# VectorE's own ordering in the edge stage: pipe drains in the place of semaphores that VectorE raises and waits for itself

## The reference

```python
# graph layer
h = layernorm(x)
neigh = segment_sum(h[src], dst, num_segments=12500)   # 200,000 edges
h = (1 + eps) * h + neigh
h = relu(h @ W1 + b1) @ W2 + b2                        # 256 -> 512 -> 256
x = x + batchnorm(h) * gamma + beta
# expert layer: top-1 of 8 experts, capacity 1.25
t = layernorm(x)
probs = softmax(t @ gate_w + gate_b); idx = argmax(probs)
x = x + prob * expert_ffn[idx](t)                      # 256 -> 1024 -> 256
```

## Time and profile before

| what | value |
|---|---|
| median of three runs | 3169.5 us |
| lowest and highest run | 3138.97 and 3172.03 us |
| span of the profiled execution | 3175.1 us |
| DVE busy | 1442.5 us (45%) |
| POOL busy | 1710.4 us (54%) |
| PE busy | 1826.2 us (58%) |
| first and last gather issue (line 791) | 118.0 and 2285.7 us |

### The profile page before, as it was taken

How to read it: one execution, slowest core, us unless ns; L and a number is a source line. 1 busy time by engine, 2 the same in 40 slices (tenths; PEclk the granted TensorE clock), 3 DMA queues, 4 the chain that set the end, 5 groups by cost and what they waited for, 6 DMA issues and landing times. The chain is left out here.

```text
span 3175.1 us, 32785 instructions
## 1 busy us (share of the span) xinstructions
PE 1826.2 (58%) x9046; PEld 1097.7 (35%) x9047; DVE 1442.5 (45%) x4225; ACT 694.9 (22%) x1116; POOL 1710.4 (54%) x1690
## 2 busy tenths in 40 slices
PE   0154444455545455655554455564568768989995
PEld 0022212222222222322222222232357645566664
DVE  8765511543225422531252112122336557786885
ACT  6600000000010001000100001110046554636642
POOL 0366664655645565555644444445315556767874
PEclk9976667676767677777877777777776688999997
DMA  7533354324633354234423332212246432222220
GB/s 244 188 104 106 116 184 138 106 88 132 197 101 91 115 182 148 87 121 144 152 65 121 120 111 65 67 54 79 54 145 216 131 93 75 71 84 73 79 83 18
DMA packets 201521, 361.08 MB, mean 114 GB/s; under 512 B 62117, under 2 KB 125947, under 8 KB 201334
## 3 DMA queue, kind: packets, MB, share of 16 engines
q0 software_dynamic: 69152, 185.00, 19.3%
q1 hardware_dynamic: 130038, 172.60, 16.8%
q10 hardware_dynamic: 2144, 1.05, 0.1%
HBM read 291.08 MB, written 71.92 MB: 114 GB/s over the span
## 5 line engine op out<-in xcount | busy, mean ns | idle before, releaser
L791 POOL DMA_INDIRECT halves<-table,halves x1240 | 1187.7, 958 | 1011.5 <-issue 367.1
L879 PE MATMUL e_sums<-halves 128*128 128x256 f16 x1920 | 334.7, 346 | 392.8 <-issue 244.1
L1062 DVE SCALAR_TENSOR_TENSOR nodes<-e_sums,above,nodes 128x256 f32 (+1 forms) x161 | 77.3, 480 | 967.0 <-remote 437.4
L879 PEld LDWEIGHTS e_sums<-halves 128*128 128x128 f16 x1920 | 229.6, 122 | 508.3 <-issue 425.7
L936 PE MATMUL e_up<-e_hT,W1s 128*128 128x512 f32 (+1 forms) x400 | 229.8, 734 | 234.9 <-ACT e_hT L985 140.2
L985 ACT ACTIVATE e_hT<-e_up 128x1024 f32<-128x1024 f32 (+1 forms) x25 | 25.2, 1007 | 1524.0 <-remote 1185.3
L1720 POOL TENSOR_TENSOR x_midl<-x_midf,x_midh 128x512 f16<-128x512 f32 x200 | 298.7, 1517 | 104.9 <-ACT x_midh L1854 99.4
L917 PE MATMUL e_tally<-w1f,counts 128*128 128x512 f16 x490 | 165.5, 480 | 281.6 <-DMA w1f<-table 204.9
L1126 DVE TENSOR_TENSOR counts<-counts,e_tally 128x490 f32 x220 | 159.8, 726 | 267.8 <-PE e_tally L907 147.9
L1810 PE MATMUL x_down<-halves,x_midh 128*128 128x256 f16 x1472 | 249.4, 277 | 16.6 <-DVE x_yb L1947 15.0
L1786 PE MATMUL x_up<-x_xTh,halves 128*128 128x512 f16 (+1 forms) x800 | 233.6, 371 | 3.1 <-ACT x_midh L1854 3.1
(11 more groups left out here) (208 smaller groups left out, 2752.4 us busy)
## 6 DMA issues: line engine op xcount, KB each, us to landing
w1f<-table SPq DMA_DIRECT2D x120, 512.0 KB
halves<-table,halves POOLq DMA_INDIRECT x1240
slot_rows<-halves SPq DMA_DIRECT2D x64, 268.0 KB
x_row<-slot_rows SPq DMA_DIRECT2D x32, 536.0 KB, 7.4
table<-halves SPq DMA_DIRECT2D x25, 512.0 KB, 2.9
counts<-in_x SPq DMA_DIRECT2D x24, 512.0 KB, 4.5
r_xin<-in_x SPq DMA_DIRECT2D x24, 512.0 KB
out<-r_row SPq DMA_DIRECT2D x24, 512.0 KB
```

The lines of the kernel that those rows point to most:

```text
L791: pool.indirect_dma_start(got[:, r, t, :], None, table.rearrange("p h d -> (p h) d"), bass.IndirectOffsetOnAxis(ap=idx[:, r, t:t + 1], axi ...
L879: ins = nc.tensor.matmul(sums[:, place, 0:D], hot[:, place, t, :], got[:, r, t, half * D:(half + 1) * D], start=(t == 0 and half == 0), st ...
```

## The change

In `stage_edges` VectorE's stream now has `dve.drain()` (the instruction DRAIN, which holds the sequencer until the engine's pipe is empty) where it waited for its own semaphores. The semaphores `s_rel`, `s_count` and `s_spread` are gone; `s_add` stays for PE. The drains stand in front of the comparisons (160), of the additions of sums (161), of the counts (220), of the folds (5), of each half of a spread (10) and of the copies of quads (25), 581 in all. In the loop and in the last addition, the drain stands in front of the wait for `s_sum`, in `gathered_once` behind it. No other engine's stream is changed, and no data instruction of DVE is added, removed or moved.

```diff
@@ gathered_once
                     nc.vector.tensor_scalar(rel[:, place, :], plan.cold[:, number * GT:(number + 1) * GT],
-                                            plan.least[:, at(number)], None, ALU.subtract).then_inc(s_rel, 1)
+                                            plan.least[:, at(number)], None, ALU.subtract)
                     word = dve.value_load(plan.words[0:1, at(number)], min_val=0, max_val=1 << 21)
                     shift = dve.snap(dve.snap(word // P) % P)
-                    dve.wait_ge(s_rel, number + 1)
+                    dve.drain()
                     for t in range(GT):
                         ins = nc.vector.tensor_scalar(hot[:, place, t, :], plan.ring[:, ring_at(shift)],
                                                       rel[:, place, t:t + 1], None, ALU.is_equal)
                     ins.then_inc(s_hot, 1)
                     dve.wait_ge(s_sum, number + 1)
-                    dve.wait_ge(s_add, number + 1)
+                    dve.drain()
                     add_window(1 - place, at(max(number - 1, 0))).then_inc(s_add, 1)
@@ gathered (the loop over windows)
-                                                ALU.subtract, ALU.subtract).then_inc(s_rel, 1)
-                        dve.wait_ge(s_rel, turn)
+                                                ALU.subtract, ALU.subtract)
+                        dve.drain()
...
                         ins.then_inc(s_hot, 1)
+                        dve.drain()
                         dve.wait_ge(s_sum, turn)
-                        dve.wait_ge(s_add, turn)
@@ count
                     dve.wait_ge(s_tile, OR + last_tile + 1)
-                    if group > 0:
-                        dve.wait_ge(s_count, group)
                     place = counts[:, :, bass.ds(column, TW)]
+                    dve.drain()
                     nc.vector.tensor_tensor(place, place, tally[:, group % BANKS, 0:KEY].rearrange("p (k d) -> p k d", d=TW),
-                                            ALU.add).then_inc(s_count, 1)
@@ fold
-                    dve.wait_ge(s_count, GROUP_OF[FIRST[u + 1] - 1] + 1)
+                    dve.drain()
@@ spread
-                    dve.wait_ge(s_add, turns)
                     for half in range(2):
+                        dve.drain()
                         for b, mask in ((0, plan.upper), (1, plan.lower)):
...
-                            then(ins)
```

More of the change, by code:

```diff
@@ L689, in stage_edges @@
         s_got = [sem(f"e_got{r}") for r in range(RG)]
-        s_hot, s_rel, s_sum, s_add, s_flush = sem("e_hot_s"), sem("e_rel_s"), sem("e_sum"), sem("e_add"), sem("e_flush")
+        s_hot, s_sum, s_add, s_flush = sem("e_hot_s"), sem("e_sum"), sem("e_add"), sem("e_flush")
         s_hrow, s_turn, s_hT, s_up, s_mid, s_down, s_h2 = (
@@ L693, in stage_edges @@
             sem("e_h2"))
-        s_tall, s_tile, s_count, s_fold, s_blank = (
-            sem("e_tall_s"), sem("e_tile"), sem("e_count"), sem("e_fold"), sem("e_blank"))
+        s_tall, s_tile, s_fold, s_blank = sem("e_tall_s"), sem("e_tile"), sem("e_fold"), sem("e_blank")
         s_part, s_used = [sem(f"e_part{h}") for h in range(2)], sem("e_used")
-        s_spread, s_cleared = sem("e_spread"), sem("e_cleared")
+        s_cleared = sem("e_cleared")
         s_pin, s_pgot, s_phot, s_psum, s_padd, s_pfree, s_prel = (
@@ L1055, in _ @@
                 last_group = counter(dve, "last_group", SINGLE - 1)
-                flushed = [0]
                 def add_window(place, group):
@@ L1104, in gathered @@
                         dve.reg_add(turn, turn, 1)
[L1106 to L1109, removed]
                 def one_hots(t):
@@ L1122, in count @@
                     dve.wait_ge(s_tile, OR + last_tile + 1)
-                    if group > 0:
-                        dve.wait_ge(s_count, group)
                     place = counts[:, :, bass.ds(column, TW)]
+                    dve.drain()
                     nc.vector.tensor_tensor(place, place, tally[:, group % BANKS, 0:KEY].rearrange("p (k d) -> p k d", d=TW),
-                                            ALU.add).then_inc(s_count, 1)
+                                            ALU.add)
                 def counted(t):
@@ L1142, in fold, with spread @@
                         count(group)
-                    dve.wait_ge(s_count, GROUP_OF[FIRST[u + 1] - 1] + 1)
+                    dve.drain()
                     wide = counts[:, :, 0:CW - P]
                     nc.vector.tensor_tensor(wide, wide, counts[:, :, P:CW], ALU.add).then_inc(s_fold, 1)
-                def spread(u, turns):
+                def spread(u):
                     first = dve.snap(dve.value_load(plan.unit[0:1, u:u + 1], min_val=0, max_val=N) // P)
                     dve.wait_ge(s_used, (u + 1) * (MIX * RG * PIECES + 1) + 2)
-                    dve.wait_ge(s_add, turns)
                     for half in range(2):
+                        dve.drain()
                         for b, mask in ((0, plan.upper), (1, plan.lower)):
                             row = blocks_of[:, block_no(dve.snap(first + b)), :].rearrange("p a d -> p (a d)")
-                            ins = nc.vector.scalar_tensor_tensor(
+                            nc.vector.scalar_tensor_tensor(
                                 out=row, in0=tally[:, BANKS - 1, half * D:(half + 1) * D], scalar=mask[:, u:u + 1], in1=row,
                                 op0=ALU.mult, op1=ALU.add)
-                            then(ins)
                 def measure(q, width=QN):
@@ L1163, in measure, with quad @@
                         nc.vector.bn_stats(stats[:, c, q * 6:q * 6 + 6], nodes[:, q, c * QN:c * QN + width])
-                def quad(q, turns):
+                def quad(q):
                     k = ORDER.index(q)
@@ L1183, in _ @@
                         if n in SPREAD and r == 0:
-                            spread(SPREAD[n], n * RG + 2 if n * RG < SINGLE else turn)
+                            spread(SPREAD[n])
                         for q in quads_at(n, r):
-                            quad(q, n * RG + r + 2 if n * RG < SINGLE else turn)
+                            quad(q)
+                dve.drain()
                 dve.wait_ge(s_sum, turn)
-                dve.wait_ge(s_add, turn)
-                then(add_window(dve.snap(dve.snap(dve.snap(turn) + 1) % 2), group_no(dve.snap(last_group))))
-                quad(NQ - 1, turn)
+                add_window(dve.snap(dve.snap(dve.snap(turn) + 1) % 2), group_no(dve.snap(last_group)))
+                quad(NQ - 1)
                 measure(NQ - 1, N - (NQ - 1) * QN)
```

## The result

In 20 runs of each kernel the kernel after took 3169.76 us in the median (3153.53 to 3200.75), the kernel before 3155.99 us (3122.79 to 3172.94). The ratio is 1.0069, with an interval of 1.0047 to 1.0091: slower by 14 us between the medians, 22 us by the ratio (15 to 29), and within one per cent. Executions over 1.5% above the fastest of their kernel, such as two of e6's twelve, count in the medians and not in the ratios. The two profiled executions show the opposite, 3159.9 us after and 3175.1 before. Single executions of one kernel lie up to 50 us apart, so two spans say nothing of a difference of this size.

A forecast was written before the change was run, and what follows sets the result against it. POOL's gathers, 1560 of 2168 us, were taken to set the stage's pace, DVE not. Costs of 4 + 5 + 1 = 10 us, less 2 to 3 for `rel` and spreads, gave 8 us on 3169.5: 3177 us, range 3145 to 3202.

The forecast's parts named there:

- What a drain does to DVE: DVE in the edge stage: drains add about 105 us of its time, between 25 and 150, not kernel time.
- (a): Behind a quad: comparisons and one to three counts come later, 0.3 us at each of 14 quads, 4 us.
- (b): In front of a quad: it starts up to 1.5 us later, 0.8 in the mean, 11 us; half counted, 5 us.
- Step (c): Last stage: DVE waits for PE there, so drains are covered; 1 us, 22 us at most without cover.
- Comparisons, quads, folds, spreads: DVE's time: comparisons 6 us, quads 5, folds and last addition under 2, spreads at most a microsecond in favour.
- Rival A: Among single-tile counts DVE becomes the bound and drains count 1:1: 3225 us, half of it 3197; chance 0.20.
- Rival B: Fewer semaphore increments shorten the "remote" pauses by a third, 36 us: 3134 us; chance 0.12.
- Rival C: All quads start into a pause, nothing reaches the path: 3165 to 3173 us; with forecast and D, chance 0.68.
- Rival D: A drain passes in 24 ns without holding the sequencer; time as before within 5 us; with forecast and C, 0.68.
- The sign to look for: POOL's waits for PE's sums (192.7 us): up by under 15 us confirms the sum, by 40 or more Rival A.

The follow-up runs named there:

- e6: Copy of the kernel after, timed beside the kernel before on the slower chip (the second comparison): 3163.7 us, ratio 1.0029 (0.999 to 1.0067).
- e4: Kernel before, no drains; counts also wait by semaphore for the one-hot row, additions for the comparisons directly in front: 2576.49 us, 1.0041 against before.
- e9: Kernel after plus two unused `bn_stats` in front of each of the 50 counts of the first 21 groups: 2582.69 us, 1.0083 against the kernel before.
- e3: Kernel after with counts and additions put back to their own semaphores, the other drains left: 2562.08 us, 0.9998 against the kernel before.
- e8: Kernel after plus one unused `bn_stats` in front of each of 157 counts away from quads, slower chip: 3190.51 us, 1.0166 against the kernel before.
- e10: Kernel after plus one unused `bn_stats` in front of each of 107 single-tile counts not near a quad: 2608.2 us, 1.018 against the kernel before.
- e1: Kernel before with drains instead of `s_count` in front of the 220 counts only: 2569.24 us, 1.0021 against the kernel before.
- e2: Kernel before with drains instead of `s_add` in front of the 161 additions of sums only: 2567.73 us, 1.0016 against the kernel before.
- e11: Kernel after plus two unused `bn_stats` in front of each of the 63 counts near quads: 2613.0 us, 1.0191 against the kernel before.
- e12: Kernel after plus two unused `bn_stats` between comparisons and addition in 95 windows without counts: 2584.86 us, 1.0083 against the kernel before.
- e5: Copy of the kernel before, unchanged, run once for a trace on the slower chip: 3127.93 us.

## Why the prediction was right, and where it was not

**The forecast.** Slower within one per cent was what came. The 8 us are met by the second comparison, 9 us (-3 to 21), and by the sum of parts on the faster chips, 9 us; in the first comparison it was 14 to 22 us, and its interval of 15 to 29 leaves 8 out. That 3177 us stands so near 3169.76 is luck in part: it starts from a median of three runs that lies 13.5 us above that of all twenty.

**What a drain does to DVE.** Each size was read off the rows of before, and held. Median gaps where DVE waited for no other engine, before and then with drain:

| place | before, us | with drain, us | difference | predicted |
|---|---|---|---|---|
| one-hot row to count | -0.08 | +0.18 | 0.26 | 0.25 |
| comparisons to addition | -0.08 | +0.21 | 0.29 | 0.25 |
| `bn_stats` to a quad's copy | -0.08 | +0.08 | 0.16 | 0.2 |
| `rel` to comparisons | 0.26 | 0.28 | 0.02 | 0.04 |

About half of the additions wait for PE's sum anyway. So 220 x 0.26 + 161 x 0.29 + 25 x 0.16 + 160 x 0.02 = 111 us at the most, against the 105 us of the prediction. DVE's busy time was said to stay nearly as before; it rose by 28 us, since instructions that no longer overlap are counted in full. That was left out.

The Trainium skill, page "VectorE: DVE Perf Modes", section "The DRAIN you can't avoid", says that a semaphore behind each instruction costs nothing extra, as the pipe is emptied between instructions anyway; it adds that an instruction that isn't held starts earlier. The runs agree with the addition and disagree with the rest: counts began 0.08 us before the end of the row in front, and e4, where a semaphore makes them wait for it, costs 1.0041 (1.0022 to 1.0061).

**What of it lies on the path.** Here the prediction's steps (a) and (b) failed in their reason, and that their sum of 9 us is near is luck. They price every quad alike, by the few drains just behind it (0.3 us) and just in front of it (up to 1.5 us, 0.8 in the mean, half of it swallowed). In the traces eleven of the fourteen quads cost nothing and those of groups 65, 108 and 114 cost 12 us together (e9 against e3). The step should have been: every count and addition between two quads lowers the rate at which lateness is made up, from 3.2 us in a group to 1.9 (10.1 less 6.9, and less 8.2, by the prediction's own numbers), and the quad that comes before it is made up hands on the rest, 8.2 us for the quad of group 65 (21.8 against 13.6). The place was right, then, and the amount came from the whole stretch in front of it. That larger doses cost as much far from the quads (e8, e10) is the other case, in which DVE is the bound.

**Step (c)**, 1 us for the last stage, was too small. From the first gather of group 120 to that of the last group it is 351.1 us in e3 and 351.0 in e1, which have no drains in front of additions, and 353.5 to 357.8 in e2, e9, e10 and e11, which have: 2 to 7 us, of the 22 that the drains could be at most there. e12, with its doses in the loop, takes 359.0.

**Comparisons, quads, folds, spreads**, at nothing to a few microseconds: right within 4 us; e3 is at 0.9998 (0.9981 to 1.0014).

**Rival A** had the mechanism: DVE among the single-tile counts, 8.2 us for a group in place of 6.9. Both numbers are in the traces (7.9 to 8.3 in e1, 6.7 to 7.3 in e3; in the kernel after 8.07 us, from 1014.75 to 1022.82, and 8.2 to 8.7 in e9's groups without doses). It also named what decides, the slack of the slot. But it priced the drains at 1:1 in the time from there on, and at 8.2 us against 10.0 the slack is built up again; the runs show most of a dose in the time only where a group reaches POOL's pace. e10 comes nearest to that price: 10.7 us for a group, and 0.6 of the dose in the time. At 8.2 us the share is 0.1.

**Rival B**, shorter pauses: "remote" 108.1 us before and 110.4 after, 105.7 and 101.8 in e5 and e6. Not seen. **Rival C**, no cost at all: excluded by the first comparison and by e1 and e2, though not by e6 alone. **Rival D**, a drain that doesn't hold: refuted by every gap.

**The sign to look for** was weak. POOL's waits for sums up by under 15 us would confirm, the prediction said. They went from 362.6 to 360.3 us in traces whose spans differ by 15 us the wrong way. The sign held, and says nothing; on a faster chip it would have been worth more, as the table shows.

No experiment pointed to a version that beats the kernel before. The best, e3, is no different from it.

## What to carry to other kernels

An ordering on the engine's own results is cheap as long as it names a result several instructions back, and dear when it waits for the one directly in front: 0.26 to 0.32 us each here, by a drain or by a semaphore alike. What that costs the kernel depends on how fast the engine makes up for a stall: compare its time for one unit of work in an unbroken run (7.9 to 8.7 us here) with the pace of the engine that sets the stage (10.0 us), and see whether the next stall comes before the last is made up. Well below that pace a tenth of the time was paid here, above it half or more.

## What the runs showed of the hardware that was not expected

Two chips gave 2564 us for the kernel before and a third gave 3150 us. The gathers in e3 (a faster chip; its time is that of the kernel before) and then in e5 (the slower chip), with what POOL waited for in front of them:

```profile
L791 POOL DMA_INDIRECT halves<-table,halves x1240: 942/949/1350, 118.0 to 1701.7; - x178
...
  issue: 363.8, 1188
  DMA halves<-rows_of: 36.0, 8
  PE e_sums L879: 14.7, 36
```

```profile
L791 POOL DMA_INDIRECT halves<-table,halves x1240: 940/946/1492, 116.5 to 2242.6; - x178
...
  issue: 363.0, 1157
  PE e_sums L879: 181.7, 19
  PEq L901: 177.6, 16
  remote: 134.6, 38
```

A gather takes the same time on both, and the pace between two is the same (363.8 and 363.0 us of issue). The waits differ: for sums 25.4 us (14.7, and 10.7 of PE's sequencer) and 359.3, "remote" none and 134.6, for the index loads 36.0 and 113.4. Together that is 546 us, the whole of the 542 us by which the gathers take longer. Neither the kernel nor the change makes this. The granted clock was 0.840 and 0.781 of full speed; PE's matmuls of line 936 took 604 and 729 ns and had 28.3 and 201.9 us of idle in front of them, so that a quad is longer there. What the "remote" pauses are, and why a quad takes longer on that chip, stays open: it was seen, not tried. Whether the drains cost more where slots are scarcer is open too: 1.0069 (1.0047 to 1.0091) in the first comparison, 1.0029 (0.999 to 1.0067) on the slower chip, 1.0035 by the sum of parts on the faster ones.
